# An expert-routed FFN on one core: x loaded by two queues, the routing preamble in two chains, code visits and a bias wait in other places

## The reference

```python
x_filtered = jnp.fft.ifft(x_spectral * spectral_gate, axis=1).real.astype(x.dtype)
x_right = hamilton(x_filtered, q_right_conj)
x_rotated = hamilton(q_left_n, x_right)
...
logits = jnp.einsum('bsd,de->bse', x, router_w) + router_b
top1 = jnp.argmax(probs, axis=-1)
for i in range(E):                      # E = 8, DIM = 256, HIDDEN = 1024
    h = jnp.einsum('bsd,df->bsf', x, w1[i]) + b1[i]
    a, g = jnp.split(h, 2, axis=-1)
    y = jnp.einsum('bsh,hd->bsd', a * jax.nn.sigmoid(g), w2[i]) + b2[i]
    out = out + jnp.where((top1 == i)[..., None], y, 0.0)
x = x + out
```

## Time and profile before

| What | us |
|---|---|
| median of 3 runs | 226.99 |
| the profiled execution, its own time | 230.32 |
| its span in the trace | 228.6 |
| TensorE busy in the span | 208.4 (91%) |
| last quarter of x landed | 13.15 |
| first matmul of tile 0 (L1025) | 40.10 |

### The profile page before, as it was taken

One profiled execution on the slowest core, in us unless ns is written; L12 is line 12 of the kernel. 1 busy time (PEld: TensorE's weight loads), 2 busy tenths in 40 slices (PEclk: granted clock), 3 DMA queues, 4 the chain that ended last, 5 costly groups with the idle time before them and its releaser, 6 DMA issues.

```text
span 228.6 us, 4308 instructions
## 1 busy us (share of the span) xinstructions
PE 208.4 (91%) x1500; PEld 192.4 (84%) x1502; DVE 159.5 (70%) x307; ACT 121.7 (53%) x204; POOL 121.9 (53%) x146
## 2 busy tenths in 40 slices
PE   7957997998899999999997997399999999999991
PEld 3727843998799999999997996299998999999991
DVE  6745954873856996598678971787698749983950
ACT  2336770254736573668465781373767456654620
POOL 5000037775700878288768777762087736840751
PEclk9999999999999999999999999679999999999997
DMA  5995523899484177918895695377707791720011
GB/s 146 342 353 190 229 80 95 288 301 352 120 252 139 46 240 157 339 36 265 235 282 189 157 303 144 114 209 161 253 23 243 164 333 57 237 52 0 23 39 36
DMA packets 31558, 41.28 MB, mean 181 GB/s; under 512 B 3112, under 2 KB 27817, under 8 KB 31402
## 3 DMA queue, kind: packets, MB, share of 16 engines
q1 hardware_dynamic: 26082, 28.32, 38.0%
q0 software_dynamic: 4512, 10.50, 18.7%
q10 hardware_dynamic: 936, 2.17, 2.4%
HBM read 36.78 MB, written 6.03 MB: 187 GB/s over the span
## 4 chain that ended last, share of the span: by engine, by line
PE 74%; issue 6%; DVE 5%; DMA 4%; another core or an unknown queue 4%; ACT 4%; SPq 1%; ACTq 1%; POOL 0%; DVEq 0%
PE y_ps L1045 9%; PE y_ps L1046 9%; PE y_ps L1047 9%; PE g_ps L1030 7%; PE g_ps L1025 7%; PE g_ps L1026 7%; PE a_ps L1030 7%; PE a_ps L1026 7%; PE a_ps L1025 7%; DMA arena<-in_x_dram 4%; DVE arena L763 1%; PE a_ps L937 1%; PE a_ps L983 1%; PE g_ps L937 1%
## 5 line engine op out<-in xcount | busy, mean ns | idle before, releaser
L376 POOL DMA_INDIRECT out_dram<-y_out,s_idx x30 | 41.2, 1374 | 52.5 <-DVE y_out L790 42.0
L518 ACT ACTIVATE arena<-g_ps,b_t 128x384 f32<-128x384 f32 (+1 forms) x64 | 34.4, 537 | 61.1 <-PE g_ps L1030 49.5
L763 DVE SCALAR_TENSOR_TENSOR arena<-a_ps,b_t,arena 128x384 f32<-128x384 f32 (+1 forms) x64 | 36.1, 565 | 41.5 <-PE a_ps L1030 27.1
L355 POOL DMA_INDIRECT xg<-x_rows,g_idx x32 | 36.7, 1147 | 40.6 <-DMA x_rows<-arena 27.8
L1045 PE MATMUL y_ps<-w_hi,u_hi 128*128 128x256 f32 x168 | 49.0, 292 | 1.1 <-DVE u_lo L769 1.0
L1046 PE MATMUL y_ps<-w_lo,u_hi 128*128 128x256 f32 x168 | 47.8, 284 | 0.0
L1047 PE MATMUL y_ps<-w_hi,u_lo 128*128 128x256 f32 x168 | 47.7, 284 | 0.0
L367 POOL DMA_INDIRECT y_out<-in_x_dram,g_idx x32 | 40.8, 1276 | 9.8 <-issue 9.8
L659 DVE TENSOR_TENSOR w_lo<-w_raw,w_hi 128x1024 fp32r<-128x1024 f32 x32 | 37.3, 1222 | 6.0 <-DMA xg<-x_rows,g_idx 4.1
L524 ACT ACTIVATE u_hi<-arena 128x384 fp32r<-128x384 f32 (+1 forms) x64 | 30.6, 479 | 14.0 <-DVE arena L763 11.0
L1025 PE MATMUL a_ps<-xr_hi,w_hi 128*128 128x256 f32 (+3 forms) x128 | 36.6, 299 | 1.6 <-DVE arena L763 1.6
(11 more groups left out here) (150 smaller groups left out, 299.0 us busy)
## 6 DMA issues: line engine op xcount, KB each, us to landing
w_raw<-in_L_ffn_w_dram SPq DMA_DIRECT2D x48, 512.0 KB
arena<-in_x_dram SPq DMA_DIRECT2D x4, 512.0 KB, 6.5
x_rows<-arena ACTq DMA_DIRECT2D x4, 512.0 KB, 3.4
b_all<-in_L_ffn_b_dram SPq DMA_DIRECT2D x1, 1024.0 KB, 5.4
xg<-x_rows,g_idx POOLq DMA_INDIRECT x32
y_out<-in_x_dram,g_idx POOLq DMA_INDIRECT x32
out_dram<-y_out,s_idx POOLq DMA_INDIRECT x30
rb_rows<-in_L_ffn_router_b_dram ACTq DMA_DIRECT2D x4, 0.0 KB
```

What stands on the lines that cost most here:

```text
L355: nc.gpsimd.indirect_dma_start(out=xg[:, s * DIM:(s + 1) * DIM], out_offset=None, in_=x_rows, in_offset=bass.IndirectOffsetOnAxis(ap=g_idx ...
L376: nc.gpsimd.indirect_dma_start(out=out_flat, out_offset=bass.IndirectOffsetOnAxis(ap=s_idx[:, i * NSUB + s:i * NSUB + s + 1], axis=0), in_ ...
L518: nc.scalar.activation(sig[:, c % SIG_RING, 0:n], pair[c % RING][1][:, 0:n], ACT.Sigmoid, bias=b1_t[:, bass.ds(e * (2 * NC) + (NC + c), 1) ...
L763: V.scalar_tensor_tensor(u32[:, c % (8 - SIG_RING), 0:n], pair[c % RING][0][:, 0:n], b1_t[:, bass.ds(e * (2 * NC) + c, 1)], sig[:, c % SIG ...
```

## The change

- **x in halves of the partitions.** Each quarter of x is loaded by two DMAs of 64 partitions each, one on SyncE's queue and one on ScalarE's. The gate's load moves to ScalarE's queue, b1's to SyncE's.
- **x_rows** is written by SyncE's queue in eight pieces, between w2's first and second half; ScalarE issues none of it.
- **Logits in two halves.** The first half of the tokens is multiplied while the last copies of `x_t` run, the bias is added to each half by itself, and the first rotation stands behind the turned logits.
- **Two chains.** VectorE's chain works out only the 32 list columns of the eight fixed tiles. GpSimd works out the spare tiles' numbers (14 small linked steps), and a second one-hot product fills the other 12 columns later.
- **Visits.** The two early visits and the one ahead of the ranks (L953) are gone from there; visits 1 to 6 stand at six places behind the loading of x. `LANDINGS` has size 3 (352 rows) in the place of size 4 (384). Landing 1 moves into the preamble.
- **Fillers.** 8 short fillers become 4; those ahead of and between the index matmuls go; of the long ones, 5 become 1 and 3, and the two between tile 0's second and third block become one.
- **Weights.** ScalarE splits w1 of expert 0 behind its last x copy, and w2 inside tile 0 as in the other tiles. VectorE's first two w1 parts no longer wait for the gathers, and b2's wait stands in `add_b2` at c = 6.

```diff
...
-    LANDINGS = (0, 1, 2, 4, 5)
+    LANDINGS = (0, 1, 2, 3, 5)
+    CONSTS = 9
...
+        def load_x(eng, half):
+
+            rows = slice(half * P // 2, (half + 1) * P // 2)
+            xv = x_flat.rearrange("(p n) d -> p n d", p=P)
+            for g in range(4):
+                eng.dma_start(x_tok[rows, 4 * g:4 * g + 4, :], xv[rows, 4 * g:4 * g + 4, :]).then_inc(x_loaded[g], 16)
...
             sp.dma_start(q_rows[0:8, :], cond).then_inc(q_loaded, 16)
-            sp.dma_start(q_rows[12:13, :], gate.rearrange("a b c j -> (a b c) j")).then_inc(q_loaded, 16)
-            xv = x_flat.rearrange("(p n) d -> p n d", p=P)
-            for g in range(4):
-                sp.dma_start(x_tok[:, 4 * g:4 * g + 4, :], xv[:, 4 * g:4 * g + 4, :]).then_inc(x_loaded[g], 16)
+            load_x(sp, 0)
+            sp.dma_start(b1_rows[:, :], b1.rearrange("e (c f) -> (e c) f", f=P)).then_inc(b1_loaded, 16)
...
             for u in range(W1U):
                 load_w1(0, u)
-            for h in range(W2U):
-                load_w2(0, h)
-
+            x_rows_v = x_rows.rearrange("(p n) d -> p n d", p=P)
+            load_w2(0, 0)
+            for b in range(NB // 2):
+                sp.wait_ge(x_rot_done, b + 1)
+                sp.dma_start(x_rows_v[:, 2 * b:2 * b + 2, :], x_rot[:, 2 * b:2 * b + 2, :]).then_inc(x_rows_written, 16)
+            load_w2(0, 1)
...
+            pool.wait_ge(consts_ready, CONSTS)
+            pool.wait_ge(cnt_ready, 1)
+            for m in range(SPARE):
+                last = G.tensor_single_scalar(over[:, m * NE:(m + 1) * NE], cnt, float((m + 1) * ITEM), ALU.is_gt)
+            link(last)
+            link(G.tensor_tensor(til, over[:, 0:NE], over[:, NE:2 * NE], ALU.add))
+            link(G.tensor_tensor(til, til, over[:, 2 * NE:3 * NE], ALU.add))
...
+            pool.sem_inc(spare_ready, 1)
+            link(G.tensor_tensor(delta, spare_end, spare_from, ALU.add))
+            link(G.tensor_tensor(of_token_en, oh[:, :].rearrange("p (e n) -> p e n", n=NB),
+                                 delta.unsqueeze(2).to_broadcast([P, NE, NB]), ALU.mult))
+            for half in (4 * NB, 2 * NB):
+                link(G.tensor_tensor(of_token[:, 0:half], of_token[:, 0:half], of_token[:, half:2 * half], ALU.add))
+            link(G.tensor_tensor(moved[:, :], of_token[:, 0:NB], of_token[:, NB:2 * NB], ALU.add))
...
+            act.dma_start(q_rows[12:13, :], gate.rearrange("a b c j -> (a b c) j")).then_inc(q_loaded, 16)
+            load_x(act, 1)
...
-            act.dma_start(b1_rows[:, :], b1.rearrange("e (c f) -> (e c) f", f=P)).then_inc(b1_loaded, 16)
-
-            for f in (0, 1, 2, 3, 4, 6):
+
+            for f in range(NB // 2 - 1):
...
-            w1_hi_part(0, 0)
             act.wait_ge(rb_loaded, GROUPS * 16)
-            act.wait_ge(logits_t_ready, 1)
-            nc.scalar.activation(logits_t[:, :], xk_ps[0][:, :], ACT.Identity, bias=rb_rows[:, 0:1])\
-                .then_inc(logits_t_done, 1)
...
+            for half in range(2):
+                cols = slice(2 * P * half, 2 * P * (half + 1))
+                act.wait_ge(logits_t_ready, half + 1)
+                nc.scalar.activation(logits_t[:, cols], xk_ps[half][:, cols], ACT.Identity, bias=rb_rows[:, 0:1])\
+                    .then_inc(logits_t_done, 1)
+
...
-                if b % 2 == 1:
-                    act.wait_ge(x_rot_done, b + 1)
-                    act.dma_start(x_rows_v[:, 2 * b - 2:2 * b + 2, :], x_rot[:, 2 * b - 2:2 * b + 2, :])\
-                        .then_inc(x_rows_written, 16)
-                if b == 0:
-                    act.wait_ge(b1_turned, 1)
-                    nc.scalar.activation(b1_t[:, :], early_ps[:, 0:P], ACT.Copy).then_inc(b1_t_done, 1)
-                if b == 2:
-                    w1_hi_part(0, 1)
-            for u in range(2, W1U):
+            act.wait_ge(b1_turned, 1)
+            nc.scalar.activation(b1_t[:, :], early_ps[:, 0:P], ACT.Copy).then_inc(b1_t_done, 1)
+            for u in range(W1U):
...
-            w2_hi_part(0)
...
-                    if c == 2 and 0 < i < NE:
+                    if c == 2 and i < NE:
                         w2_hi_part(i)
...
-            w1_lo_part(0, 0)
...
-            V.tensor_copy(cnt, totals)
-            V.scalar_tensor_tensor(over, totals.unsqueeze(2).to_broadcast([P, NE, SPARE]), 1.0 / ITEM,
-                                   iota[:, 1:SPARE + 1].unsqueeze(1).to_broadcast([P, NE, SPARE]),
-                                   ALU.mult, ALU.is_gt)
             link(V.tensor_tensor(pos_en, cum_en, base.unsqueeze(2).to_broadcast([P, NE, NB]), ALU.add))
-            link(V.tensor_reduce(til, over, AX.X, ALU.add))
-            link(V.tensor_tensor_scan(spare_end, ones[:, 0:NE], til, 0.0, ALU.mult, ALU.add))
-            link(V.tensor_tensor(spare_from, spare_end, til, ALU.subtract))
-            link(V.scalar_tensor_tensor(delta, spare_from, float(ITEM), spare_at[:, :], ALU.mult, ALU.add))
-            link(V.scalar_tensor_tensor(ahead_en, pos_en, float(ITEM), delta.unsqueeze(2).to_broadcast([P, NE, NB]),
-                                        ALU.is_ge, ALU.mult))
-            link(V.tensor_tensor(pos[:, :], pos[:, :], ahead[:, :], ALU.add))
...
+            V.tensor_copy(r_f[:, :], slot_r[:, :])
+            V.tensor_single_scalar(q_at[:, :], slot_q[:, :], 1.0, ALU.mult)
+            link(V.tensor_scalar(past[:, :], slot_q[:, :], float(NSUB), float(BIG), ALU.is_ge, ALU.mult))
+            link(V.tensor_tensor(q_at[:, :], q_at[:, :], e_from[:, :], ALU.add))
+            slot_one_hot(0)
+            link(V.tensor_tensor(q_fixed[:, :], q_at[:, :], past[:, :], ALU.add))
...
             dve.wait_ge(idx_summed, 1)
-            V.tensor_scalar(g_idx[:, :], idx_ps, -1.0, 0.0, ALU.add, ALU.max).then_inc(idx_ready, 1)
-            link(V.tensor_scalar(idx_f[:, 0:TS], idx_ps, 0.0, float(BIG), ALU.is_equal, ALU.mult))
-            V.scalar_tensor_tensor(s_idx[:, :], idx_ps, -1.0, idx_f[:, 0:TS],
-                                   ALU.add, ALU.add).then_inc(s_idx_ready, 1)
-
+            indices(early_ps[:, 0:FX], 0, FX)
+            subtile_one_hot(q_oh_spare, FX, TS - FX, q_spare).then_inc(q_oh_spare_ready, 1)
+
+            dve.wait_ge(spare_ready, 1)
...
+            dve.wait_ge(idx_spare_summed, 1)
+            indices(turn_ps[0][:, 0:TS - FX], FX, TS - FX).then_inc(s_idx_ready, 1)
...
+                if i == 0:
+                    dve.wait_ge(b2_loaded, 16)
...
                 if i == 0:
+                    w1_lo_part(0, 2)
                     w1_lo_part(0, 3)
-                    w2_lo_part(0)
-                    dve.wait_ge(b2_loaded, 16)
...
-                    if c == 4 and 0 < i < NE:
+                    if c == 4 and i < NE:
                         w2_lo_part(i)
...
-            for s in range(2):
-                dve.wait_ge(gathered[s], 16)
+            w1_lo_part(0, 0)
             w1_lo_part(0, 1)
-            w1_lo_part(0, 2)
...
-            visit(1)
...
-            keep_warm(early_ps, 8)
-            visit(2)
+            keep_warm(early_ps, 4)
...
-                if f == 3:
+                if f == 5:
...
-            pe.wait_ge(b1_loaded, 16)
-            T.transpose(early_ps[:, 0:P], b1_rows[:, :], ident[:, :]).then_inc(b1_turned, 1)
+            def logits(half):
+
+                for k in range(KH):
+                    tokens = x_t[:, k, half * 8 * P:(half + 1) * 8 * P].rearrange("p (j a t) -> p a j t", j=2, a=GROUPS)
+                    for a in range(GROUPS):
+                        last = T.matmul(xk_ps[half][a * COLS:(a + 1) * COLS, half * 2 * P:(half + 1) * 2 * P],
+                                        wr_rot[:, k * COLS:(k + 1) * COLS], tokens[:, a],
+                                        start=(k == 0), stop=(k == KH - 1))
+                last.then_inc(logits_t_ready, 1)
...
             pe.wait_ge(wr_ready, 1)
-            pe.wait_ge(x_t_done, 6)
-            pe.wait_ge(x_t_done_v, 2)
-            for k in range(KH):
-                for g in range(GROUPS):
-                    last = T.matmul(xk_ps[0][g * COLS:(g + 1) * COLS, :], wr_rot[:, k * COLS:(k + 1) * COLS],
-                                    x_t[:, k, g * 512:(g + 1) * 512], start=(k == 0), stop=(k == KH - 1))
-            last.then_inc(logits_t_ready, 1)
-            visit(3)
+            pe.wait_ge(x_t_done, 4)
+            logits(0)
+            pe.wait_ge(x_t_done, 7)
+            pe.wait_ge(x_t_done_v, 1)
+            logits(1)
...
+            for g in range(NB // GROUPS):
+                if g == 2:
+                    visit(1)
+                pe.wait_ge(logits_t_done, g // 2 + 1)
+                last = T.transpose(late_ps[:, g * P:(g + 1) * P], logits_t[:, g * P:(g + 1) * P], ident[:, :])
+            last.then_inc(logits_ready, 1)
...
             pe.wait_ge(rot_ready, KH)
-            rotate_blocks(0)
-            pe.wait_ge(logits_t_done, 1)
-            for j in range(NB // GROUPS):
```

(40 more changed lines are left out.)

102 lines of the change are left out of this document (69 added, 33 removed).

## The result

The changed kernel takes 236.62 us, the median of 4 runs (235.29 to 237.41). The kernel before, beside it on the same chip, takes 228.11. The ratio is 1.039, with a 95% interval of 1.029 to 1.049: **slower**, where the prediction said 2.8 us faster. A ratio here leaves out executions more than 1.5% above the fastest of their kernel, and a median is that of all of them. The profiled execution took 235.29 us, with a span of 233.6.

A forecast was written before the change was run, and what follows sets the result against it. The start of the first product, behind x's load, x_rows writes and gathers, was taken as the bound. T = 12.2 with T+25.1 put it at 37.3 against 40.10, 2.8 us less: from 226.99 to 224.2 us, range 221.8 to 227.4.

The forecast's parts named there:

- the other way round, over TensorE alone: Second sum to the first product over TensorE's own work: lists, visit 4, fillers, index product, turns; gave T+25.0.
- T+25.1: First product's start, summed as gathers at T+17.1 plus 8.0 us from gathers to product; 37.3 us against 40.10.
- a visit of 2 us in the open: Listed sign that the prediction would be wrong: a visit that long with no wait to cover it.
- T, the load of x: T is the landing of x's last quarter; forecast 12.2 us (10.5 to 13.5), 0.95 us earlier than before.
- x alone at that rate would be in at ... 9.4: Early bound for loading x: 351 GB/s from 5 us on; with about 1 us to the wait, 10.5.
- half the ports, slower: Rival: pieces of 64 partitions move at half of 351 GB/s, x lands at 16, total 228.0 us; chance 0.10.
- The brake: ScalarE issues x pieces and gate before its table load, up to 3 us; holds T at some 11.5 in effect.
- Logits and ranks: VectorE's first look at the logits at T+4.5, 1.2 us less through halved logits; ranks pass at T+6.95.
- Gathers and lists: Gathers released by x_rows writes at T+17.1, 1.4 us less; index lists ready at T+14.4, over 2 us ahead.
- Gathers beside w1 parts: Two gathers slowed beside VectorE's w1 parts cost 1.0 us, fillers cover half; price 0.5 (0 to 1.5).
- The clock: Rival: TensorE's clock falls between T+12.6 and the end of visit 4; +2 us, about 226.0; chance 0.15.
- Tile 0 and behind: From first product on, b2's wait, w2's split and landings cost 0; tiles stay 188 us long, code layout 1 us either way.

The follow-up runs named there:

- e4: Changed kernel with visits and landings where they stood in the kernel before, size 384 in the landings again; ratio to the kernel before 1.007.
- e1: Changed kernel without visits 5 and 6 and their two landings; ratio to the kernel before 1.042.
- e6: Changed kernel with x in whole quarters on SyncE's queue and visits where they stood before; ratio to the kernel before 1.013 [0.993, 1.034].
- e13: The text of e6 measured again in another set; ratio to the kernel before 1.013 [1.001, 1.025].
- e17: e13 with the fourth visit after the fourth rotation step; median 230.95 us beside 229.74 for the kernel before, no ratio.
- e18: e13 with the third visit after x's second turn and the fourth in the third's place; ratio to the kernel before 1.015.
- e10: Changed kernel with x's eight half pieces all on SyncE's queue; ratio to the kernel before 1.030, median 225.78 us.
- e7: Kernel before with only x loaded in halves on two queues, gate and b1 moved as in the change; ratio to the kernel before 1.040.
- e9: Changed kernel with wr issued ahead of x on ScalarE's queue; ratio to the kernel before 1.024, median 223.26 us.
- e3: Changed kernel with x in whole quarters on SyncE's queue, gate and b1 on the queues of before; ratio to the kernel before 1.010.
- e11: Changed kernel with whole quarters of x, two on each queue, wr behind ScalarE's; ratio to the kernel before 1.011, median 220.30 us.
- e8: Kernel before with only the visits and landings placed as in the change; ratio to the kernel before 1.021.
- e14: e13 with the fourth visit behind the index products instead of ahead of the ranks; ratio to the kernel before 1.063.
- e5: The changed kernel measured again, nothing altered; ratio to the kernel before 1.033.
- e2: Changed kernel with the short fillers of before, 8 early and those around the index products; ratio to the kernel before 1.040.
- e12: Changed kernel with x in whole quarters on SyncE's queue and no visit or landing at all; ratio to the kernel before 1.032.
- e15: e3 with the sixth visit ahead of x's first turn and the fifth behind the fourth; 231.17 to 240.18 us, median 235.9, no ratio.
- e16: The changed kernel measured a third time; 236.53 to 242.16 us, median 240.6, beside 230.0 for the kernel before, no ratio.

## Why the prediction was wrong

The product was forecast at 37.3 and came at 45.97, 8.7 us late: 2.0 us of it stand ahead of the gathers, 6.7 behind them.

**The step that failed most is "the other way round, over TensorE alone"**, which put the product at T+25.0 and so confirmed T+25.1. It counted visit 4, at up to 2.9 us, and put visits 5 and 6 at nothing, without a reason, though they stand in the same stretch; they took 3.95 and 3.09 us. It also left out the 3.3 us of sequencer steps between the load of the control word and the first turn (37.9 to 41.18). Before they took 3.6 us (32.5 to 36.09) and ran beside the landing of the gathered rows; they cost at most 1.0 us there (4.37 us from gather to turn, against 3.36 where the rows are what TensorE waits for, e4). With them the first turn stands 9.88 us behind the gathers, before 4.37, and gathers to product becomes 14.67 us in place of 8.0; the rest of the difference is the clock, below. Where both visits stand elsewhere the predicted 8.0 is nearly right: 8.01 (e1), 8.49 (e4), 7.65 (e6), 8.35 (e13), 8.04 (e17), 8.67 (e18). The prediction had the row with a visit of 2.9 us and priced it for visits 1, 2 and 4 only. Its own sign of being wrong, "a visit of 2 us in the open", is what came.

**T, the load of x, failed as well.** It was forecast at 12.2, 0.95 us earlier; the last quarter is turned from 13.56, later than before (13.28). The first half of the failure is in the rate: "x alone at that rate would be in at ... 9.4" took 351 GB/s for pieces of 64 partitions too. It is 224 to 259 (e10, e7, e9, after), so that against whole quarters (e3, e11) the first look at the logits comes 2.4 to 5.3 us later. The start was off too: T = 13.15 is that of one profile, whose execution took 3.3 us more than the median. In the eight other profiles with whole quarters and no visit in the way (e3, e6, e8, e11 to e14, e17) the last quarter is turned from 10.60 to 11.82, in that of before from 13.28. The rival "half the ports, slower" had this mechanism, with a chance of 0.10. Its rate of a half was too hard, and its 228.0 us held only the load. The Trainium skill's sentence in the prediction ("SBUF — State Buffer", section "Can I just issue two DMAs to hit both halves?", two DMAs for the two halves gain 6% over one) warned rightly: e10 and e11 show that one transfer over all partitions is the fast one. The prediction had not asked either what lies behind x on ScalarE's queue. wr does; it landed at 13.05 us, before 3.1 us behind its issue at 1.42, and in e7 it holds TensorE for 4.56 us. In the changed kernel that order costs at most the 0.70 us of its wait, and moving it brought nothing (e9).

**The brake** by ScalarE's square root showed (VectorE's reciprocal at 8.35 in place of 5.92), but it was not what ended last.

**Logits and ranks.** First look T+4.5 = 16.7 forecast, 19.25 measured: T is 0.9 us late, and turns and logits ran at the 1.2 GHz level (the four turns of a step 0.97 and 1.06 us in place of 0.71). (The terms of that sum add to about T+4.3.) The mechanism was right: where the clock stayed at 1.00 the look comes 4.2 us behind the start of the last turns (e3, e5, e9, e11), before 5.6, and 5.7 with the clock at half. So the gain of the halved logits is 1.4 us, and the clock took it back. Ranks forecast at 19.15, measured 21.48: 2.2 us behind the first look, 2.45 forecast. Visits 1 and 2 took 0.32 and 0.38 us, as priced.

**Gathers and lists.** From first look to gathers 12.6 us were forecast, 12.05 measured, before 12.88. The gathers wait for the x_rows writes, as said, and `g_idx` is ready 1.9 us ahead. So the two chains do what they should; the gain is under 1 us, because x_rows bounds them and not the lists.

**Gathers beside w1 parts.** The second gather took 1.92 us beside VectorE's split at 32.67, twice the 1.0 of its neighbours: the price of 0.5 to 1.5 was right, and hidden behind the visits.

**The clock** fell, as that rival has it, but at other places: after the waits for x (half level from 13.8 to 17.2 us), beside visits 5 and 6 (30.9 to 37.7) and again from 41.1 to 44.5. It costs 1.4 us at the logits and 1.6 us from the first turn to the product (4.79 in place of the 3.15 that the prediction reckons with, and that e9 and e11 show); the six filler passes, 4.47 us long, end before the sequencer is through. What it was that let the clock fall is not shown: e5, the same kernel, has no fall at 14. In e2 more fillers didn't repair the later one.

**Tile 0 and behind** at 188 us came out at 187.6. That is in part luck: before and after both hold pauses that the sets with little scatter don't have (177.3 there).

**What stays open.** With both causes undone the product starts at 38.97, 39.88 and 36.44 (e6, e13, e17), and no ratio shows a version faster than the kernel before. Part of that needs no further cause. For the kernel before in the sets at 218.5 us, an estimate from e3, e4 and e9 to e11 puts the product at 39.5: 218.5 less 1.7 (time over span) less 177.3 (product to end), if its tiles take as long as theirs. Against 39.5 the products of e6 and e13 gain next to nothing, and that of e17 gains 3 us, which fits its fastest execution alone. In these three profiles it is 20.8, 21.2 and 22.3 us from the first product to the next tile's turn (14.4 in e3, e9, e10 and e11), but those executions took 5.0, 8.5 and 11.0 us more than the fastest of their kernel, so they can't speak for it. Why TensorE pauses in them was not found. Both causes together were never undone in a set with little scatter, and neither was the changed kernel itself measured in one. The 8.5 us between the medians are also more than the 5.0 us between the two profiled executions; the profiled execution of before took 3.3 us more than the median of 226.99, with x late, and what else differs lies in runs that no profile shows.

## What to carry to other kernels

A branch to a far place in the code had a price of its own here, 0.3 us or 2 to 7 us: put it where the engine waits anyway and in the order of the code, and count every one that stands in a stretch before you sum over that stretch. Removing it only moved the pause to the first use (e1, e12). A load cut over the partitions was slower on one queue and on two, so keep a load over all partitions whole, and look at what small load is queued behind the big one. When two ways of summing agree, check that both contain all instructions of the stretch: the agreement here was that of two incomplete sums. And when a forecast starts from one profile, ask how far its legs vary: T did by 1.5 us and more.

## What was not expected of the hardware

- Pieces of 64 partitions: 224 to 259 GB/s at a DMA share of 1.02 to 1.05, whole quarters 351 to 391 (before, e3, e11), on one queue or two. The same 4 KB packets take 1.4 to 1.8 times as long.
- A DMA queue of kind "instruction", by its times TensorE's, moves seven packets of 16 KB, nine (e15) and fourteen (e14) where landings were visited out of order; single branches took up to 7.20 us (e18).
- The same kernel takes 218.5 us in some sets and 229 to 230 us in others, on one and the same chip by the listing (e9 to e12, e13 to e16); in the latter TensorE pauses in later tiles by 1.6 to 3.6 us without a releaser.
